# Dot products of gathered and looked-up embeddings: the layout of the vectors in SBUF, and which engine empties the turned parts

## The reference

```python
e = jnp.stack([tbl_0[ids[:, 0]], ..., tbl_25[ids[:, 25]]], axis=1)
T = jnp.concatenate([r_dense[:, None, :], e], axis=1)        # 512 x 27 x 128
Z = jnp.einsum('bnd,bmd->bnm', T, T)
z = Z[:, iu0, iu1]                                            # pairs n < m
h = jnp.concatenate([z, r_dense], axis=1)
h = jnp.maximum(h @ W_top1 + b_top1, 0.0)                     # 479 x 512
h = jnp.maximum(h @ W_top2 + b_top2, 0.0)                     # 512 x 256
y = h @ W_top3                                                # 256 x 1
```

## Time and profile before

| | us |
|---|---|
| median of 3 runs | 114.56 |
| lowest and highest | 114.41, 114.81 |
| the profiled execution | 115.23 |
| its span | 113.4 |

### The profile page before, as it was taken

How to read it: one execution, slowest core, us unless ns; L and a number is a source line. 1 busy time by engine, 2 the same in 40 slices (tenths; PEclk the granted TensorE clock), 3 DMA queues, 4 the chain that set the end, 5 groups by cost and what they waited for, 6 DMA issues and landing times.

```text
span 113.4 us, 3721 instructions
## 1 busy us (share of the span) xinstructions
PE 101.9 (90%) x1564; PEld 84.9 (75%) x1564; DVE 85.4 (75%) x181; ACT 78.8 (69%) x196; POOL 67.6 (60%) x71
## 2 busy tenths in 40 slices
PE   4988999997998996979599989989979997999992
PEld 4956865875786873759389787976979996997990
DVE  4599999999999999993494883883948869591110
ACT  5179999999999969954462996781937868462111
POOL 2777878877687777777767776777777300000000
PEclk9999999999999999999958999999999999999999
DMA  3899895774858779931221222122222100000000
GB/s 51 238 314 360 301 320 137 267 238 138 263 134 299 208 243 388 377 128 39 62 52 52 66 54 53 46 69 52 52 56 65 49 6 3 6 6 0 0 0 1
DMA packets 6119, 14.72 MB, mean 130 GB/s; under 512 B 1995, under 2 KB 1995, under 8 KB 5974
## 3 DMA queue, kind: packets, MB, share of 16 engines
q1 hardware_dynamic: 4034, 10.27, 28.2%
q0 software_dynamic: 2048, 4.20, 12.7%
q10 hardware_dynamic: 20, 0.02, 0.1%
HBM read 14.48 MB, written 0.00 MB: 128 GB/s over the span
## 4 chain that ended last, share of the span: by engine, by line
DVE 42%; PE 40%; issue 10%; ACT 5%; POOL 1%; DVEq 0%; POOLq 0%
DVE onehot L428 25%; PE mlp_ps L327 12%; PE dots L301 10%; DVE hot_low L435 9%; PE mlp_ps L339 5%; DVE pairs L193 4%; ACT pairs L516 4%; PE turned L285 4%; PE mlp_ps L317 3%; PE mlp_ps L271 3%; DVE vecs L171 2%; PE turned L352 2%; DVE vecs L170 2%; PE mlp_ps L347 1%; ACT h_sb L564 1%
## 5 line engine op out<-in xcount | busy, mean ns | idle before, releaser
L241 POOL DMA_INDIRECT gathered<-table,rows x64 | 66.9, 1045 | 20.8 <-issue 19.2
L428 DVE TENSOR_TENSOR onehot<-mlp_ps,hot_rows_sb 128x1536 fp32r<-128x1536 f32 x20 | 34.2, 1750 | 1.2 <-PE mlp_ps L252 1.2
L516 ACT ACTIVATE pairs<-dots 32x80 f32<-32x80 f32 (+3 forms) x112 | 25.6, 228 | 8.9 <-PE dots L301 7.0
L193 DVE COPY pairs<-dots 32x80 f32<-32x80 f32 (+3 forms) x112 | 25.8, 230 | 7.7 <-PE dots L301 5.4
L271 PE MATMUL mlp_ps<-onehot,hot_high 128*128 128x512 f32 (+1 forms) x88 | 24.5, 404 | 3.3 <-DVE onehot L428 2.7
L271 PEld LDWEIGHTS mlp_ps<-onehot,hot_high 128*128 128x128 f32 x88 | 15.1, 197 | 10.2 <-DVE onehot L428 5.2
L271 PE MATMUL mlp_ps<-onehot,hot_low 128*128 128x512 f32 (+1 forms) x88 | 20.4, 374 | 0.3 <-DVE hot_low L435 0.3
L327 PE MATMUL mlp_ps<-pairs,w1p_sb 128*128 128x128 f32 x160 | 20.2, 275 | 0.0
L327 PEld LDWEIGHTS mlp_ps<-pairs,w1p_sb 128*128 128x128 f32 x160 | 19.0, 192 | 0.0
L271 PEld LDWEIGHTS mlp_ps<-onehot,hot_low 128*128 128x128 f32 x88 | 15.3, 188 | 3.7 <-DVE hot_low L435 0.5
L301 PE MATMUL dots<-vecs 128*32 128x27 f32 x1024 | 13.7, 199 | 2.0 <-DVE vecs L171 0.8
(11 more groups left out here) (34 smaller groups left out, 58.4 us busy)
## 6 DMA issues: line engine op xcount, KB each, us to landing
hot_sb<-hot_table SPq DMA_DIRECT2D x10, 512.0 KB, 4.0
wide_ids<-hot_ids SPq DMA_DIRECT2D x10, 256.0 KB, 4.7
w1p_sb<-w_pairs SPq DMA_DIRECT2D x1, 1280.0 KB, 8.3
gathered<-table,rows POOLq DMA_INDIRECT x64, 4.0
w_sb<-w SPq DMA_DIRECT2D x1, 512.0 KB
dense_sb<-dense_t SPq DMA_DIRECT2D x1, 256.0 KB, 9.7
w1d_sb<-w_dense SPq DMA_DIRECT2D x1, 256.0 KB, 10.4
ids_sb<-ids_and_base SPq DMA_DIRECT2D x1, 36.0 KB, 1.9
```

What stands on the lines that cost most here:

```text
L193: copied = copy(dst, cols.rearrange("p g t -> p t g"))
L241: nc.gpsimd.indirect_dma_start(gathered[:, h, c, :], None, table, bass.IndirectOffsetOnAxis(rows[:, h, c:c + 1].bitcast(u32), 0),).then_in ...
L428: nc.vector.tensor_tensor(onehot[:, f % 2, k:k + n, :], ids_ps(f).unsqueeze(1).to_broadcast([P, n, B]), hot_rows_sb[:, k:k + n].unsqueeze( ...
L516: return nc.scalar.activation(dst, src, ACT.Copy)
```

## The change

`vecs` is laid out as `[half, vector, sample]`: a vector's 64 samples of a half are side by side, a sample's 32 vectors are 64 elements apart. The turned parts have that order in PSUM already, so `evacuate` copies straight through. The found values and the dense vector go to runs of 64. TensorE's dot products read weights and moving side with a step of 64 elements. During the look-ups ScalarE empties all four parts, where VectorE emptied two; from part 4 on the engines alternate as before, and TensorE waits for the counts of both.

```diff
-        vecs = sb("vecs", [P, HALVES, HALF // 4, 4, QUAD])
+        vecs = sb("vecs", [P, HALVES, QUAD, HALF])
...
         def found(f):
-            return mlp_ps[:, f % 2, :].rearrange("p (h j g) -> p h j g", h=HALVES, j=4)
+            return mlp_ps[:, f % 2, :].rearrange("p (h s) -> p h s", h=HALVES)
...
+        BEHIND = len(TURN_AT)
+        def out_by_dve(n):
+            return max(0, (n - BEHIND + 1) // 2)
+        def out_by_act(n):
+            return n if n <= BEHIND else BEHIND + (n - BEHIND) // 2
         def evacuate(copy, n):
             half, k = divmod(n, PARTS)
-            src = turned[:, n % 2, 0:PART * P].rearrange("p (f j g) -> p j g f", j=4, g=HALF // 4)
             at = k * 2 * PART
             if k == 0:
-                copy(vecs[:, half, :, :, V:QUAD].rearrange("p g j f -> p j g f"), src[:, :, :, 0:COPIES])
-            return copy(vecs[:, half, :, :, at:at + 2 * PART].rearrange("p g j f -> p j g f"), src)
+                copy(vecs[:, half, V:QUAD, :].rearrange("p f s -> p (f s)"), turned[:, n % 2, 0:COPIES * HALF])
+            return copy(vecs[:, half, at:at + 2 * PART, :].rearrange("p f s -> p (f s)"), turned[:, n % 2, 0:PART * P])
...
         def column(col):
-            return vecs[:, :, :, :, col].rearrange("p h g j -> p h j g")
+            return vecs[:, :, col, :]
...
                 n = half * PARTS + k
                 if n >= 2:
-                    pe.wait_ge((vecs_dve, vecs_act)[n % 2], n // 2)
+                    if out_by_dve(n - 1):
+                        pe.wait_ge(vecs_dve, out_by_dve(n - 1))
+                    pe.wait_ge(vecs_act, out_by_act(n - 1))
...
                 n = (h + 1) * PARTS
-                pe.wait_ge(vecs_dve, (n + 1) // 2)
-                pe.wait_ge(vecs_act, n // 2)
+                if out_by_dve(n):
+                    pe.wait_ge(vecs_dve, out_by_dve(n))
+                pe.wait_ge(vecs_act, out_by_act(n))
...
-                        sample = vecs[:, h, g, j, :]
+                        sample = vecs[:, h, :, j * GROUPS + g]
...
             for f in range(NH):
                 look_up(f)
-                if f - 1 in TURN_AT:
-                    turned_out(*TURN_AT[f - 1])
...
             def turned_out(half, k):
                 n = half * PARTS + k
-                if n % 2 == 1:
+                if n % 2 == 1 or n < BEHIND:
                     act.wait_ge(turned_ready, n + 1)
                     evacuate(copy, n).then_inc(vecs_act, 1)
```

More of the change, by code:

```diff
@@ L577, in _ @@
                     act.wait_ge(dense_in, 16)
-                    copy(column(DENSE), dense_sb[:, :].rearrange("p (h j g) -> p h j g", h=HALVES, j=4))
+                    copy(column(DENSE), dense_sb[:, :].rearrange("p (h s) -> p h s", h=HALVES))
                 if f - 1 in TURN_AT:
```

## The result

The change makes the kernel slower: 116.88 us (median of 4, 115.60 to 117.31) against 114.48 (114.18 to 114.81) for the kernel before beside it, a ratio of 1.019 with a 95% interval of 1.015 to 1.023. The profiled execution took 117.03 us with a span of 115.2, 1.8 more than before.

The account below looks back on a forecast made before the run. VectorE was taken to bound the look-ups and TensorE what follows. Terms of -2.0, -0.2 and +0.1 us summed to -2.1, taking the median from 114.56 to 112.5 us (own range 112.0 to 113.2; 8 in 10: 112.0 to 118.8).

Parts of the forecast that it names:

- Bounds: Whole kernel: VectorE's time prices the look-ups, TensorE's what follows from about 51 us on.
- Part 1: Look-ups f = 3 and f = 7: VectorE loses two evacuations, 1.00 us each, gain 2.0 us on the path.
- Part 2: Look-ups: ScalarE gains two evacuations (+1.8 us) but loses scattered writes (about -4); path cost 0, at most 0.2 us each.
- Part 3: End of look-ups: the last weights may land late for TensorE, now coming at 49.97; 0 to 1.0 us, taken as 0.1.
- Part 4: Before the dense matmul: ScalarE's copy of 256 found values falls from 613 ns to about 0.39 us, saving 0.2 us.
- Part 5: Dot products: TensorE's reads 256 bytes apart cost 0; upper bound 13.6 us for 1024 records.
- Rival 1: Dot products: stepped reads cost TensorE 3.5 to 7.4 us, say 5.5, giving 118.0 us; chance 0.37.
- Sum: Whole kernel: -2.0 - 0.2 + 0.1 = -2.1 us; profiled execution 113.1 us, median 112.5 (112.0 to 113.2).
- Gathers keeping up by 0.6 us: Half 7's transposes: wanted at 91.5, last gather issued at 88.3 and landed at 90.9, so gathers still keep up.
- Rival 2: Gain given back by late weights (1.0 us), ScalarE's late one-hots (0.4) or TensorE's half clock; about 113.8 us, chance 0.10.

Follow-up runs that it names:

- contiguous reads: The changed kernel, but dot products read contiguous numbers of the same half (so other products); 113.02 us, ratio 0.986 to the kernel before.
- runs of 2 again: Second run of the changed kernel with pairs of samples side by side (a sample's vectors 8 bytes apart); 113.41 us, ratio 0.990 to the kernel before.
- evacuations alone again: Second run of the kernel before with its old layout, only ScalarE emptying all four parts; 113.39 us, ratio 0.989 to the kernel before.

## Why the prediction was wrong, point by point

The forecast was 112.5 us and faster at 0.53; measured was 116.88, the first rival's side, within the range of 112.0 to 118.8.

- **Bounds (VectorE first, TensorE after)**: right as far as the look-ups go. Every stretch without evacuations is 4.46 or 4.47 us.
- **Part 1, -2.0 us**: right to 0.01 us. `hot_low` of f = 9 started at 47.75 instead of 49.74 (the traces of both).
- **Part 2, ScalarE**: right. Found values 585 ns (forecast 615), the two moved copies 0.91 us (0.9), `hot_high(4)` at 23.30 (23.1), no wait of TensorE at f = 4.
- **Part 3, weights**: right, no wait at 49.97 (0.1 us forecast).
- **Part 4, `last_found(1)`**: 404 ns (forecast 390), and its wait is gone; with it 0.6 us of the way to the first layer (0.2 forecast).
- **Part 5, stepped reads at 0**: the step that failed. The choice rested on "this read goes at about half the pace of TensorE's fastest here, which leaves it room", and on reads from PSUM. Undisturbed halves took 2.48 us instead of 1.26, weights and moving side each paid (0.76 and 0.45 us a half), and the time lost 3.9 us. Pace in elements was the wrong measure: the step of 8 bytes has the same pace and is free. Lines of 16 bytes, of which a contiguous read of 4-byte numbers needs one in four elements and a step of 16 bytes or more a new one each time, fit what was measured. The reads from PSUM did not carry over: ScalarE and VectorE copy from PSUM with a step of 256 bytes as fast as without (611 and 680 ns against 607 and 685), TensorE from SBUF does not. Whether the memory or the engine makes that difference no run tells. The one row on SBUF with a step of 16 bytes or more was ScalarE's scattered write (1.78 against 0.88 ns), and it spoke for the price.
- **Rival 1**: the mechanism and nearly the size: 3.5 to 7.4 us forecast, 3.9 measured (against the kernel with contiguous reads). Two of its terms were off and cancelled. It let loads and streams overlap, 0.92 us a half; they add, 1.21, though an element costs 0.74 and 0.52 ns and not 0.90. And it let 3.9 us hide in the holes, of 7.4; of 8 x 1.21 = 9.7 us 5.8 were hidden. By first to last start the halves took 18.7 us against 14.9 with contiguous reads, 3.8 more and not 8 x 1.15 = 9.2, so 5.4 of it was hidden in holes.
- **Sum without part 5**: the kernel with contiguous reads is the forecast's kernel, 113.0 us against 112.5 (112.0 to 113.2). Its profiled execution took 113.24 where the sum said 113.1, so the terms were right to 0.1 us in total. That was in part luck: the holes grew by 1.5 us, and the half clock, which the sum left in, was gone. The rest of the 0.5 us is the step from the profiled execution to the median, 0.67 us, which was taken over unchanged.
- **Gathers keeping up by 0.6 us**: they keep up by nothing. TensorE wants the last part at 91.5 as forecast (contiguous reads), but the last gather is issued at 88.8 and not 88.3. Of the five executions in the table that gain, three wait at that part for it: 0.23 us (contiguous reads), 0.38 (runs of 2 again) and 0.14 (evacuations alone again). Why the issue did not keep its time stays open.
- **Rival 2 (gain given back)**: weights and one-hots did not give it back. The half clock did fall differently, but to the gain's side in the trace. What gave back 0.7 of 2.0 us are the holes, which none of its three ways had.

## What to carry to other kernels

A layout that makes the writer's runs long makes the reader's steps wide; price both sides, and look for a step that serves both: two float32 side by side were enough here for ScalarE's writes (628 against 1068 ns) and free for TensorE's reads. Where no row shows a kind of access, rows on another memory are weak evidence even if their direction is the same; here the row on the same memory, though a write of another engine, was the better guide. Time won ahead of a stage counts only as far as that stage's own limits let it, here the supply of TensorE's instructions and behind it the gathers.

## What the runs showed of the hardware

- TensorE's reads from SBUF of float32 with a step of 16 bytes or more take 1.8 to 2.0 times as long for short matmuls (2.11 us with 16 bytes and 2.39 with 256 against 1.18, for 128 weight loads). At 256 bytes the weights have 0.76 of the 1.21 us and the moving side 0.45, and the two add; with a step of 8 bytes they cost nothing (1.19).
- ScalarE's copy of 512 float32 to SBUF takes 1068 ns if each lands 512 bytes from the next and 628 if two lie side by side; from four on it is 580 to 585.
- TensorE can stand without a wait that shows. All 23 such stretches of over 0.35 us, the longest 1.45, ended 1.30 to 1.61 us after a packet of 16 KB of instructions had landed. Slower or fewer instructions both take the holes out of the halves: at 2.5 us a half the last five have none, and with 128 instructions in 0.9 us no half has one. 256 instructions in 1.1 us do not always make one: the last half has none in any kernel.
